# A GNN layer on one core: two of the four dense lists multiplied as rounded high and low parts

## The reference

```python
xn = _layernorm(x, axis=-1)
gathered = edge_weight[:, None] * xn[src]                      # 200,000 x 256
agg = segment_sum(gathered, dst, num_segments=6250) + node_vec1
x = x + agg + linear_attention(xn)
x = x + top2_of_8_experts(_layernorm(x, axis=-1))
```

## Time and profile before

| | before |
|---|---|
| median of 3 runs | 2530.46 us (2526.78 to 2535.07) |
| the profiled execution | 2506.26 us, its span 2504.5 us |
| TensorE (PE) busy | 2195.2 us, 88% |
| VectorE (DVE) busy | 1781.8 us, 71% |
| GpSimd (POOL) busy | 1465.3 us, 59% |
| ScalarE (ACT) busy | 1280.1 us, 51% |
| mean granted TensorE clock | 0.932 |

### The profile page before, as it was taken

How to read it: one execution, slowest core, us unless ns; L and a number is a source line. 1 busy time by engine, 2 the same in 40 slices (tenths; PEclk the granted TensorE clock), 3 DMA queues, 4 the chain that set the end, 5 groups by cost and what they waited for, 6 DMA issues and landing times. The chain is left out here.

```text
span 2504.5 us, 46512 instructions
## 1 busy us (share of the span) xinstructions
PE 2195.2 (88%) x16549; PEld 1900.3 (76%) x16550; DVE 1781.8 (71%) x3160; ACT 1280.1 (51%) x2683; POOL 1465.3 (59%) x1342
## 2 busy tenths in 40 slices
PE   7987899898998899989999999998889945999993
PEld 4656678777877788777877778777777744999993
DVE  7989977777776777776777777777656657555552
ACT  2225445554554455545555455545433345888872
POOL 4760366666666666666656666566655503788883
PEclk9998899999999999999999999999999967999997
DMA  5542422232222222322222222222334453555555
GB/s 144 146 129 76 144 80 78 77 92 80 80 76 89 78 80 76 89 81 80 83 85 81 84 82 85 76 83 79 94 106 135 140 187 52 81 82 82 83 83 132
DMA packets 160939, 235.96 MB, mean 94 GB/s; under 512 B 54834, under 2 KB 121805, under 8 KB 160490
## 3 DMA queue, kind: packets, MB, share of 16 engines
q0 software_dynamic: 70896, 164.43, 26.1%
q1 hardware_dynamic: 75536, 55.29, 8.1%
q10 hardware_dynamic: 14314, 13.68, 1.6%
HBM read 186.46 MB, written 53.24 MB: 96 GB/s over the span
## 5 line engine op out<-in xcount | busy, mean ns | idle before, releaser
L834 POOL DMA_INDIRECT picked<-xn_dram,place x1029 | 1058.9, 1029 | 771.8 <-PE bank L932 328.6
L1054 ACT COPY stage<-bank 128x512 f32<-128x512 f32 x343 | 200.7, 585 | 741.6 <-remote 567.7
L932 PE MATMUL bank<-picked,pick_w 128*128 128x256 f32 x2058 | 512.0, 383 | 8.7 <-issue 8.2
L932 PEld LDWEIGHTS bank<-picked,pick_w 128*128 128x128 f32 x2058 | 397.8, 194 | 71.7 <-issue 16.1
L928 PE MATMUL bank<-window,stage 128*128 128x256 f32 x1568 | 415.0, 408 | 12.8 <-issue 8.6
L928 PEld LDWEIGHTS bank<-window,stage 128*128 128x128 f32 x1568 | 300.3, 202 | 58.9 <-issue 18.7
L920 PE MATMUL bank<-hot_w,hots 128*128 128x128 bf16 x4116 | 314.7, 228 | 29.5 <-issue 27.0
L1060 ACT ACTIVATE pick_w<-hots,weights 128x128 f32<-128x128 bf16 x1029 | 338.6, 397 | 0.0
L1369 DVE TENSOR_TENSOR hot_w<-hots,bank 128x1536 bf16<-128x1536 bf16 x343 | 327.1, 954 | 11.9
L920 PEld LDWEIGHTS bank<-hot_w,hots 128*128 128x128 bf16 x4116 | 272.4, 103 | 69.6 <-issue 36.8
L1201 DVE TENSOR_TENSOR vals<-hot_t,field_rep 128x1666 bf16<-128x1666 bf16 x150 | 156.4, 1043 | 217.0 <-remote 198.7
(11 more groups left out here) (262 smaller groups left out, 3430.4 us busy)
## 6 DMA issues: line engine op xcount, KB each, us to landing
picked<-xn_dram,place POOLq DMA_INDIRECT x1029
w<-in_L_ffn_W_dram SPq DMA_DIRECT2D x16, 512.0 KB, 8.6
xn_dram<-xn ACTq DMA_DIRECT2D x49, 128.0 KB, 2.0
xT_dram<-xT ACTq DMA_DIRECT2D x49, 128.0 KB, 2.2
base_dram<-acc SPq DMA_DIRECT2D x7, 896.0 KB
sum_dram<-acc SPq DMA_DIRECT2D x7, 896.0 KB
z_dram<-vals SPq DMA_DIRECT2D x7, 896.0 KB
out_dram<-sum_dram SPq DMA_DIRECT2D x1, 6250.0 KB, 22.3
```

What stands on the lines that cost most here:

```text
L834: pool.indirect_dma_start(out=picked[:, i % SETS * PICK + q, :], out_offset=None, in_=xn_dram, in_offset=bass.IndirectOffsetOnAxis(ap=plac ...
L932: mm = pe.matmul(sum_ps[pp], pick_w[i % SETS][:, q, :], picked[:, i % SETS * PICK + q, :], start=False, stop=(q == PICK - 1))
L1054: act.copy(block_sb[pp].rearrange("p j c -> p (j c)"), banks[pp][:, :]).then_inc(a_copied, 1)
```

## The change

Of the 4 dense lists the last 2 (`SPLIT`; the other two are `FULL`) are multiplied in another number format. A block B is rounded to fp32r (`high_block`), the rest B - high is kept as `low_block`; the same is done with the source rows (`high_win`, `low_win`). In place of one fp32 product per list there are three fp32r products: high block x high rows, high block x low rows, low block x high rows.

- ScalarE: `evacuate` makes two copies of 128x256 in place of one of 128x512 (the split half first, with rounding). `raise_window` rounds the source rows once in a group.
- VectorE: `lower_block` once a step (128x256: PSUM bank minus `high_block`), at the end of the step's list, before `add` of the last step. `lower_window` once a group (128x512).
- TensorE: a step's products begin with the 4 of the high blocks, then 2 fp32 products of the other lists, then the 3 picked ones, and end with the 2 of the low blocks, which wait for `lowered`. `blocks` waits for `lowered` of two steps earlier as well, since VectorE now reads the bank too. Once a group there is a wait for `lower_window`.

```diff
+    SPLIT = DENSE // 2
+    FULL = DENSE - SPLIT
@@ TensorE, blocks
                 pe.wait_ge(a_copied, t + 1)
+                pe.wait_ge(lowered, t + 1)
@@ TensorE, rows
-                for j in range(DENSE):
-                    pe.matmul(sum_ps[pp], block_sb[pp][:, j, :], window[par][:, j, :], start=(j == 0), stop=False)
+                for j in range(SPLIT):
+                    pe.matmul(sum_ps[pp], high_block[pp][:, j, :], high_win[par][:, j, :], start=(j == 0), stop=False)
+                    pe.matmul(sum_ps[pp], high_block[pp][:, j, :], low_win[par][:, j, :], start=False, stop=False)
+                for j in range(FULL):
+                    pe.matmul(sum_ps[pp], block_sb[pp][:, j, :], window[par][:, j, :], start=False, stop=False)
                 pe.wait_ge(pick_done, t + 2)
                 pe.wait_ge(rows_in[i % SETS], 16 * PICK * uses(i, u))
                 for q in range(PICK):
-                    mm = pe.matmul(sum_ps[pp], pick_w[i % SETS][:, q, :], picked[:, i % SETS * PICK + q, :], start=False, stop=(q == PICK - 1))
+                    pe.matmul(sum_ps[pp], pick_w[i % SETS][:, q, :], picked[:, i % SETS * PICK + q, :], start=False, stop=False)
+                pe.wait_ge(lowered, t + 3)
+                for j in range(SPLIT):
+                    mm = pe.matmul(sum_ps[pp], low_block[pp][:, j, :], high_win[par][:, j, :], start=False, stop=(j == SPLIT - 1))
                 mm.then_inc(o_done, 1)
@@ TensorE, unit
                 pe.wait_ge(window_in[par], 16 * (turn + 1))
+                if k == 0:
+                    pe.wait_ge(kv_step, 5 + g)
@@ ScalarE, evacuate
-                act.copy(block_sb[pp].rearrange("p j c -> p (j c)"), banks[pp][:, :]).then_inc(a_copied, 1)
+                act.copy(high_block[pp][:, :, :].rearrange("p j c -> p (j c)"), banks[pp][:, FULL * P:DENSE * P])
+                act.copy(block_sb[pp][:, 0:FULL, :].rearrange("p j c -> p (j c)"), banks[pp][:, 0:FULL * P]).then_inc(a_copied, 1)
+
+            def raise_window(g):
+                act.wait_ge(window_in[g % 2], 16 * (g // 2 + 1))
+                act.copy(high_win[g % 2][:, :, :], window[g % 2][:, FULL:DENSE, :]).then_inc(kv_made, 1)
@@ ScalarE, begin and unit
+                raise_window(0)
+                    if more and k == GRP - 2 and i == 2:
+                        raise_window(g + 1)
@@ VectorE
+            def lower_block(t, pp):
+                dve.wait_ge(a_copied, t + 3)
+                dve.tensor_tensor(low_block[pp][:, :, :].rearrange("p j c -> p (j c)"), banks[pp][:, FULL * P:DENSE * P],
+                                  high_block[pp][:, :, :].rearrange("p j c -> p (j c)").bitcast(F32), ALU.subtract).then_inc(lowered, 1)
+
+            def lower_window(g):
+                dve.wait_ge(kv_made, 4 + g)
+                dve.tensor_tensor(low_win[g % 2][:, :, :], window[g % 2][:, FULL:DENSE, :], high_win[g % 2][:, :, :].bitcast(F32), ALU.subtract).then_inc(kv_step, 1)
@@ VectorE, begin
                 hots(1, 1, None)
+                lower_window(0)
+                lower_block(0, 0)
@@ VectorE, unit, at the end of each of the 7 steps
+                    if more and k == GRP - 1 and i == 3:
+                        lower_window(g + 1)
+                    if i + 1 < BU:
+                        lower_block(t + i + 1, (odd + i + 1) % 2)
+                    elif after:
+                        lower_block(t + BU, 1 - odd)
                 add(BU - 1)
```

More of the change, by code:

```diff
@@ L678, in edge_sum @@
         window = [sb("window0", [P, DENSE, D]), stage[:, 0:DENSE * D].rearrange("p (t d) -> p t d", d=D)]
+        high_win = [sb(f"high_win{i}", [P, SPLIT, D], F32R) for i in range(2)]
+        low_win = [sb(f"low_win{i}", [P, SPLIT, D], F32R) for i in range(2)]
+        high_block = [sb(f"high_block{i}", [P, SPLIT, P], F32R) for i in range(2)]
+        low_block = [sb(f"low_block{i}", [P, SPLIT, P], F32R) for i in range(2)]
         block_sb = [stage[:, DENSE * D + i * DENSE * P:DENSE * D + (i + 1) * DENSE * P].rearrange("p (j c) -> p j c", c=P) for i in range(2)]
@@ L739, in edge_sum @@
         o_done = sem("o_done"); o_added = sem("o_added")
-        listed = sem("listed"); split = sem("split"); pick_done = sem("pick_done"); rows_in = [sem(f"rows_in{i}") for i in range(SETS)]
+        listed = sem("listed"); split = sem("split"); lowered = sem("lowered"); pick_done = sem("pick_done"); rows_in = [sem(f"rows_in{i}") for i in range(SETS)]
         block = ctx.enter_context(nc.Block())
@@ L841, in _ @@
             pe.sem_inc(logit, 2)
+            pe.sem_inc(lowered, 2)
             def turn_z(n):
```

## The result

The changed kernel takes 2556.98 us (median of 4, 2551.69 to 2564.22), the kernel before beside it 2529.36 us (2526.78 to 2535.07): ratio 1.0109, 95% interval 1.0092 to 1.0126. It is 28 us slower where I had forecast 16 us of gain. Two later measurements of the same two kernels gave 1.0073 (1.0050 to 1.0095) and 1.0087 (1.0056 to 1.0118). The profiled execution took 2551.69 us, its span 2549.9 us, at a mean granted clock of 0.923 (before: 0.932).

A forecast was written before the change was run, and what follows sets the result against it. TensorE was taken to bound undisturbed steps, with VectorE's chain almost as long between stalls. Gains of 12 us (sorting units) and 7 (last group) less 3 (`lower_window`, longer start) made 16: 2530 to 2514 us, range 2484 to 2562.

The forecast's parts named there:

- The bound in a clean step and its gain: TensorE bounds an undisturbed step of 3.74 us; six fp32r matmuls for four fp32 records gain 0.14, giving 3.60 us.
- No cost at the format switches: At two new switches between fp32r and fp32 inside a TensorE step: 0 to 0.08 us each, taken as 0.
- ScalarE's and VectorE's new durations: Per step, ScalarE's one copy of 585 ns becomes two of 370 ns; VectorE's `lower_block` takes 417 ns.
- The gain of a clean step in the last group: In the last group, a step of 4.33 us at TensorE's pace gains 0.14 us.
- The step that failed: Stall at each unit's start: ends about 10.3 us after the table's start, not tied to the rows' work; hides work inside.
- The mid-unit waits: TensorE's fifth set of blocks waits 1.4 us for VectorE's `hot_w` in a third of units, which lose 0.3 us each.
- my 12: Gain in us over the 42 units of the sorting groups: 14 x (-0.3) + 14 x 0.85 + 14 x 0.3.
- The last group: No sorting on VectorE there, steps at TensorE's pace: 49 x 0.14 = 7 us gain.
- Rival 3: Each unit's stall lengthens with TensorE's instruction count: 18 us, 2532; chance 0.24 together with VectorE eating the whole gain.
- Rival 2: VectorE's new wait and work behind `lower_block` bound every unit, fifth `hot_w` late: 2560, far end 2576 us; chance 0.25.
- slower: Whole kernel slower by more than 0.3%, 7.6 us: rival 2 and the upper edge of VectorE eating the gain; chance 0.28.

The follow-up runs named there:

- e10: The kernel before, unedited, run again for a profile on the same occasion as the changed kernel: 2506.30 us.
- e11: The changed kernel, unedited, run again on one occasion with the kernel before: 2526.12 us against 2507.72, ratio 1.0073.
- e2: Changed kernel with all four dense products fp32 again; copies, subtraction and waits stay, the difference unused: 2535.81 us, 1.0113 of before.
- e3: Changed kernel without the two products of the low blocks, all else kept: 2488.89 us, 0.9939 of before.
- e15: Changed kernel; in a unit's seventh step TensorE waits ahead of the last products for VectorE's addition of the step before: 2523.96 us, 1.0071 of before.
- e1: Kernel before with two more unused pairs of weight load and matmul at the head of each step's products: 2531.22 us against 2507.87, 1.0090.
- e13: Kernel before with the base's 34 matmuls issued seven at a time between the first step's fp32 products: 2561.69 us, 1.0212.
- e16: Kernel before with 34 more unused matmuls of the base's shape behind a unit's fourth step: 2587.73 us, 1.0338.
- e4: Kernel before with the 34 base matmuls after a unit's third step in place of its first: 2557.93 us, 1.0225.
- its two halves: Kernel before with only the two copies of 256 columns: 2537.98 us, 1.0031; with only VectorE's subtraction and its waits: 2534.72 us, 1.0018.
- e8: Changed kernel with VectorE's subtraction placed behind the addition of the step before: 2531.49 us, 1.0005 of before.
- e17: The same kernel as e8, changed kernel with the subtraction behind the addition, on another occasion: 2556.32 us against 2506.43, 1.0195.

## Why the prediction was wrong

**Right.** The bound in a clean step and its gain: 3.61 us for 3.60. No cost at the format switches. ScalarE's and VectorE's new durations. The gain of a clean step in the last group, 0.16 us for 0.14. TensorE never waits noticeably for `lowered`, and for `hot_w` in 14 places, 8.3 us in all.

**The step that failed** stands in the first part: that a stall's end "seems tied to the start of the table, about 10.3 us after it", and that what is done inside is hidden. I took it as a constant and let every saving outside it count whole. In before the end holds for most units (34 of 41 in e10); under the change it doesn't: in 16 units of e11 the stall ends later than 11.3 us, in the long unit above 15.1 us behind the table. In this trace pair from one occasion the excess of the two steps grew from 5.62 to 6.71 us a unit, pauses and low clock together. 1.09 us are 45 us over 41 units, about as much as all clean steps save. The excess grew when ScalarE and VectorE got the change's work (e2), but not when TensorE had less to do beside it (e3), and it was smaller behind pauses of about 1.4 us (e15); work taken from TensorE showed in the time by less than half (e3 against e2).

**The mid-unit waits** were the second term: steps three to five hold 0.39 us more than before's in place of the 0.98 - 12/41 = 0.7 us that my sum let VectorE eat. The mechanism was there, smaller than I made it. Without the stall's growth the units would have gained (0.98 - 0.39 - 0.09) x 41 = 20 us, near my 12.

**The last group** was a third, small miss. I took its clean step for all 49: 7 us. Over the whole group the gain is 1.5 us (249.0 to 247.5), and 2.6 in the pair e10 and e11 (250.1 to 247.5). Its steps are 5.2 us apart on average, before and after, since 14 of before's 48 and 21 of the changed kernel's take over 4.5 us.

**The rivals.** Rival 3 named the right place, a longer stall, with the wrong cause and too small a size: e1 refutes the number of instructions. Rival 2 had the sign, by a late VectorE at the fifth `hot_w`, which the waits don't show; its price of 2560 came near the result for the wrong reason. I gave slower 0.28, and what I lacked was a rival in which savings themselves are taken back. The trace of before held a hint: two units in a row, whose two steps begin at 1283 and 1317 us, took 12.9 and 13.9 us for the same work. A stretch with such a spread isn't a constant to build on.

**Open.** What the stall is. TensorE's pauses of 0.75 us' rhythm come with the lower clock, which sets in some us after the first of them, and both change with what TensorE did ahead of them (e13, e15, e16). That would fit something that holds the engine back, but nothing here shows what, and e4 and e13 speak against a simple rule: moving or thinning out the base made it worse. The Trainium skill ("NOTIFIC — the notification-queue block", section "7.1 Overflow: three behaviours, one of which stalls the engine") says that the block's internal pipeline always holds back rather than lose a record inside the block, and that in one of its settings a full ring stalls the producer; by that a dense run of short instructions could stall an engine. No run here shows it, and e1, whose steps issue four instructions more, speaks against it. The loading of instructions shows no tie to the stall: in e10 the queue of kind instruction (q8; which engine it serves isn't told) moves 83 packets in the 41 units, at all distances from the table, while the stall comes at one place of each. Nor is it shown why e2 has more long units than its two halves, why e3 has hardly any, or why one kernel has 2 of them on one occasion and 18 on another. Whether the kernel before would also get a pause for nothing wasn't tried: both pauses put there came out too small in nearly all units. No variant that computes the whole result beat the kernel before beyond its interval.

## What to carry to other kernels

If an engine's timeline has stretches in which it idles for nothing that the trace shows, cut the whole loop into its steps over many iterations before pricing a change, and look whether that stretch is a constant; a saving elsewhere is worth its face value only if it is. A cheap test is to put a pause into a clean step: if the time stays, one may doubt that shortening the step will bring anything (here that was seen in the changed kernel alone, after the fact). Where one kernel's ratio moves by 1 to 2% between occasions, compare only within one occasion, run the reference point of every argument on it with a trace, repeat the verdict on another, and look whether counts from the trace (here the long units) move with the ratio.

## What the runs showed of the hardware that I had not expected

In a stall TensorE starts one to five short matmuls every 0.72 to 0.76 us (1279.80 to 1286.50 us in the long unit), and at the lower clock fp32r matmuls stand 0.21 us apart in place of 0.12 (1288.32 to 1288.53 us there). One run of 34 short matmuls draws a pause inside it, 0.56 us in the one shown (e16). With a mean pause of 1.36 us in it a unit took 35.76 us, without it 35.70 on another occasion, and had 1.4 us less of low clock (e15, e11). One kernel ran at 1.0005 and at 1.0195 of before on two occasions (e8, e17).
